# Second attention: transposed scores, attending and outputs of a head one slot later

## What is computed

```python
x = layernorm(x + L0_attn(x))      # 16 heads of 64, keys and values from a latent of 64, causal
x = layernorm(x + L0_ffn(x))       # shared expert + 2 of 16 routed experts
x = layernorm(x + L1_attn(x))      # 16 heads of 16 features; the change is here
x = layernorm(x + L1_ffn(x))       # relu^2, then 5 steps of a spiking neuron, mean of the spikes
```

```python
q_c = rms_norm(xh @ W_DQ.T @ W_UQ.T, q_norm_w); q = concat(q_c, q_c @ W_QR.T)    # 16 + 64
k_c, v = split(xh @ W_DKV.T @ W_UKV.T);         k = concat(rms_norm(k_c, k_norm_w), xh @ W_KR.T)
attn = softmax(q @ k.T * 16**-0.5 + causal);    out = (attn @ v) @ W_O.T
```

## Time and profile before

| | us |
|---|---|
| median of 3 runs | 1758.01 (1756.82 to 1760.86) |
| profiled execution | 1759.73 |
| its span, first to last instruction | 1757.8 |
| PE busy in the span | 1607.7 (91%) |
| DVE busy | 1201.9 (68%) |
| ACT busy | 1015.7 (58%) |
| POOL busy | 461.5 (26%) |
| mean granted TensorE clock | 0.969 of full |

### The profile page before, as it was taken

How to read it: one execution, slowest core, us unless ns; L and a number is a source line. 1 busy time by engine, 2 the same in 40 slices (tenths; PEclk the granted TensorE clock), 3 DMA queues, 4 the chain that set the end, 5 groups by cost and what they waited for, 6 DMA issues and landing times. The chain is left out here.

```text
span 1757.8 us, 29390 instructions
## 1 busy us (share of the span) xinstructions
PE 1607.7 (91%) x9060; PEld 1115.9 (63%) x9060; DVE 1201.9 (68%) x4134; ACT 1015.7 (58%) x2544; POOL 461.5 (26%) x843
## 2 busy tenths in 40 slices
PE   7899999999999999987799976889899988899996
PEld 4667676767677676753588744656556655466765
DVE  1787888888887878755655457788888776125345
ACT  1686766766676767633434364667677766643340
POOL 1000101010101010100275376667676643200001
PEclk9999999999999999998899978999999999999998
DMA  4211111212111111102055528788788786000000
GB/s 107 77 31 47 38 49 43 49 39 52 37 49 43 49 38 40 38 7 96 15 174 162 131 66 155 136 141 150 123 146 134 117 123 119 1 7 24 12 24 30
DMA packets 82632, 128.47 MB, mean 73 GB/s; under 512 B 14640, under 2 KB 40704, under 8 KB 82352
## 3 DMA queue, kind: packets, MB, share of 16 engines
q1 hardware_dynamic: 71232, 100.11, 28.6%
q0 software_dynamic: 9664, 25.93, 5.7%
q10 hardware_dynamic: 1584, 0.55, 0.2%
HBM read 73.59 MB, written 35.65 MB: 62 GB/s over the span
## 5 line engine op out<-in xcount | busy, mean ns | idle before, releaser
L416 ACT ACTIVATE c_probs<-c_probs,a_negmax 128x128 f32<-128x128 f32 (+3 forms) x512 | 279.6, 550 | 0.0
L2004 DVE CUSTOM_DVE_ANT_0 a_junk<-a_ps_score,c_mask 128x128 f32<-128x128 f32 (+3 forms) x512 | 220.3, 487 | 76.1 <-PE a_ps_score L1633 68.2
L1853 ACT ACTIVATE c_probs<-a_ps_st 128x384 f32<-128x384 f32 (+1 forms) x384 | 191.5, 530 | 125.9 <-PE a_ps_st L1655 124.2
L421 ACT ACTIVATE c_probs<-a_ps_trans 128x512 f32<-128x512 f32 (+1 forms) x256 | 124.7, 487 | 215.0 <-PE a_ps_trans L334 214.0
L476 DVE CUSTOM_DVE_ANT_0 c_probs<-a_ps_score,c_mask 128x128 f32<-128x128 f32 (+3 forms) x512 | 219.7, 485 | 19.6 <-PE a_ps_score L318 18.6
L334 PE MATMUL a_ps_trans<-c_ident,c_probs 128*128 128x128 f32 x1280 | 188.7, 278 | 17.8 <-DVE c_probs L493 16.1
L334 PEld LDWEIGHTS a_ps_trans<-c_ident,c_probs 128*128 128x128 f32 x1280 | 147.3, 141 | 87.4 <-issue 39.3
L1655 PE MATMUL a_ps_st<-a_qs,a_ks 128*128 128x512 f32 (+3 forms) x512 | 153.8, 371 | 40.7 <-ACT c_probs L1853 20.4
L539 POOL TENSOR_SCALAR a_rstd<-a_mv 128x4 f32<-128x4 f32 x8 | 1.8, 230 | 704.6 <-DVE a_mv L506 704.6
L317 PE MATMUL a_ps_score<-a_kh,a_qs 128*128 128x128 f32 (+3 forms) x512 | 167.4, 351 | 6.9 <-issue 4.5
L493 DVE TENSOR_SCALAR c_probs<-c_probs,a_recip 128x128 f32<-128x128 f32 (+3 forms) x512 | 164.4, 384 | 4.5
(11 more groups left out here) (273 smaller groups left out, 3156.1 us busy)
## 6 DMA issues: line engine op xcount, KB each, us to landing
a_qs<-a_qlow SPq DMA_DIRECT2D x128, 128.0 KB, 2.2
bounce<-a_words SPq DMA_DIRECT2D x64, 256.0 KB, 6.2
a_qs<-bounce SPq DMA_DIRECT2D x128, 128.0 KB, 5.7
a_ks<-bounce SPq DMA_DIRECT2D x128, 128.0 KB, 6.2
slot_out<-m_y SPq DMA_DIRECT2D x80, 128.0 KB, 2.0
a_xT<-in_xT SPq DMA_DIRECT2D x8, 512.0 KB, 3.8
c_X<-in_x SPq DMA_DIRECT2D x8, 512.0 KB
token_rows<-c_X SPq DMA_DIRECT2D x8, 512.0 KB, 5.7
```

The lines of the kernel that those rows point to most:

```text
L416: act.activation(at, at, ACT.Exp, scale=-1.0, bias=negmax[:, n % 4, i:i + 1], accum_out=rowsum[:, n % 4, i:i + 1]).then_inc(s_exp, 1)
L421: act.activation(probT[:, n % 4, TGCOL[grp]:TGCOL[grp] + TGLEN[grp]], ps_trans[(3 * n + grp) % 2][:, 0:TGLEN[grp]], ACT.Copy).then_inc(s_p ...
L1853: act.activation(probT[:, r8, col:col + width], ps_st[item % 2][:, 0:width], ACT.Exp).then_inc(s_stc, 1)
L2004: dve.tensor_tensor_reduce(out=junk[:, to:to + keys], in0=ps_score[g][:, at:at + keys], in1=C.mask[:, L - keys:L], scale=-1.0, scalar=3.0e ...
```

## The change

`BACK` goes from 7 to 8: the transposed scores of a head, and with them ACT's exponentials and POOL's cut, run eight slots behind its scores. Attending, the copy `yq`, the transposition back and the outputs of a quad are each called one slot later than before, on PE, ACT and DVE. Where SP issues its fills is not edited, but `used(u)` counts items that are now issued a slot later. `turn_max`, `keep_max` and `shifts` stay at slot 4u + 5.

```diff
-BACK = 7
+BACK = 8
@@ PE
-                    if n >= 12 and n % QUAD == 0 and (n - 12) // QUAD < NQUADS:
-                        attend((n - 12) // QUAD, (0,))
-                    if n >= 12 and n % QUAD == 1 and (n - 13) // QUAD < NQUADS:
-                        attend((n - 13) // QUAD, (1, 2, 3))
+                    if n >= 13 and n % QUAD == 1 and (n - 13) // QUAD < NQUADS:
+                        attend((n - 13) // QUAD, (0,))
+                    if n >= 13 and n % QUAD == 2 and (n - 14) // QUAD < NQUADS:
+                        attend((n - 14) // QUAD, (1, 2, 3))
...
-                    if n >= 12 and n % QUAD == 2 and (n - 14) // QUAD < NQUADS:
-                        turn_back((n - 14) // QUAD)
+                    if n >= 13 and n % QUAD == 3 and (n - 15) // QUAD < NQUADS:
+                        turn_back((n - 15) // QUAD)
@@ ACT
-                    if n >= 12 and n % QUAD == 2 and (n - 14) // QUAD < NQUADS:
-                        u = (n - 14) // QUAD
+                    if n >= 13 and n % QUAD == 3 and (n - 15) // QUAD < NQUADS:
+                        u = (n - 15) // QUAD
                         act.wait_ge(s_y, u + 1)
@@ DVE
-                    if n >= 12 and n % QUAD == 3 and (n - 15) // QUAD < NQUADS:
-                        outputs((n - 15) // QUAD)
+                    if n >= 13 and n % QUAD == 0 and (n - 16) // QUAD < NQUADS:
+                        outputs((n - 16) // QUAD)
```

## The result

| | before | changed |
|---|---|---|
| median of 22 runs, us | 1758.82 (1753.79 to 1764.51) | 1765.02 (1760.35 to 1773.44) |
| ratio to before, 95% interval | | 1.0034 [1.0024, 1.0045] |
| profiled execution, us | 1759.73 | 1768.87 |
| its span, us | 1757.8 | 1767.0 |
| PE busy, us | 1607.7 | 1614.4 |

The change costs 6.2 us by the medians and 9.2 by the two spans; the profiled execution of the changed kernel is the second slowest of its 22, whose granted clock has a median of 0.972. The predicted 1759 is missed by 6; 1765.0 lies inside the range of 1745 to 1770. Measured again on another chip the change came out at 1.0014 [0.9997, 1.0030], so its size is uncertain by a few us.

The account below looks back on a forecast made before the run. PE sets the pace, idling for the DMA of the shifts and for ACT. Terms -5.5 - 5 + 0.5 + 6 + 5 - 1.4 + 1.5 = +1.1 us on the median 1758.0 gave 1759 us; range 1745 to 1770.

Parts of the forecast that it names:

- Part 1: Middle of attention: later need for the shifts takes off 5.5 us of waits and 5 of lost clock.
- rival C: Second attention: fill, words and shifts all come a slot later, waits and slow clock stay; +11, 1769 us; chance 0.20.
- Part 2: ACT's queue: the moved yq copy delays copies PE waits for; 0.5 us per eight slots, +6 over 12 periods.
- Part 3: DVE's queue: outputs behind max, means and mix make PE's attend block wait 8 times about 0.6 us, +5.
- Part 4: Start of the stage: PE runs slot 8's scores within the 6.13 us wait, landing unchanged at 1100.8 us; -1.4.
- The late phase: After the front has ended: three quads wait about 1.05 us each for keys, probably one clock drop; net +0.5.
- Part 5: Tail: one head's exponents move there, and ACT waits for the attending of quad 30 in slot 134; +1.5 us.
- B: Relief: shift waits after the start and lost clock behind them end, new holes are half; -13, 1745 us; chance 0.23.
- D: Fills: the 1.3 us margin for a quad's own keys and queries is not there; 1780 us; chance 0.10.
- the signs named ahead: Shift waits behind the start under 2 us, slot 3's hole near 1.0, eight DVE waits about 0.6, three late key waits.
- the clock's one drop: Sign for 1130 to 1420 us: granted TensorE clock at 1.00 but for one drop.

Follow-up runs that it names:

- the other trace: The changed kernel as it is, run and profiled again on another chip: 1.0014 of the kernel before, median 1766.28 us.
- the last version with `BACK` 7: The changed kernel with ACT's yq copy, DVE's outputs and SP's word stores reordered and BACK at 7: 0.9927 of the kernel before, median 1748.65 us.

## Why the prediction was right and wrong, point by point

**Part 1, shift cover and fills: the waits stayed, and this carries the miss.** Predicted -5.5 us of waits and -5 of clock in the middle. Measured: waits 4.7 to 4.4 us, 3.5 in the other trace; clock lost 6.8 to 5.1 us (13.6 and 10.2 us at half clock), 1.7 in the other trace; by the runs with half the loads the two together went from 9.0 to 9.4, in the other trace to 5.7. So 0 to 3.3 us in place of 10.5. The clock is the milder half of this: over all executions on the other chip 7.2 us of it came back in the whole kernel. Why, with the waits hardly smaller, isn't shown.

The step that failed is the claim that a longer period gives the DMA queue time, so that the shift waits go. The queue doesn't run on the period; it runs from a fill's release to the need of the shifts behind it. That is four slots in both kernels. Before: slots 3 to 6, 2.98 + 2.86 + 5.30 + 2.49 = 13.6 us, and 0.7 into the next slot. Changed: slots 4 to 7, 2.14 + 6.15 + 2.91 + 2.52 = 13.7, and 0.7. The period did grow by 1.5 us (25.6 to 27.1): slots 2 and 3 by some 2, slots 0 and 1 shrank by 1.3, and slots 4 to 7 grew by 0.8 to 0.9. But the stretch gave up slot 3, of 2.98 us, for slot 7, of 2.1 to 2.3 before the change, and that took back what slots 4 to 7 had gained.

The DMA side is no shorter than before. SP in the changed kernel and the landing of the shifts of the last row, which answer to the earlier trace rows:

```profile
1335.93 0.50 SPq L1434 DMA_DIRECT2D a_qs<-a_qs  x1
...
1341.33 0.53 SPq L1447 DMA_DIRECT2D a_qs<-a_shift  x1
```

```profile
DMA to landing us min/median/max: 9.2/9.2/9.2
```

The shifts leave earlier behind their fill, 5.4 us after its first issue in place of 6.9, as forecast, and land later, 9.2 us in place of 7.0: 14.6 us in all against 13.9 (medians over the eleven of the middle: 14.1 and 13.6). Leaving earlier was worth nothing here: the same loads and stores stand ahead of them in the queue.

The count of slots orders the other runs too. The four slots take 15.1 us in the run with the old `BACK` (waits in the middle 0.4 us), 13.7 in the changed kernel (4.4), 13.6 in the one before (4.7), 13.4 with ACT's copy moved (5.9), 13.2 with DVE's outputs moved (6.1) and with `BACK` alone (5.3), 12.8 with both moved (7.9), while fill and shifts take 13.6 to 14.1 us wherever their landing is recorded. With the stores behind the shifts that is 12.4 to 12.7 us, and the waits are 0.8 us at 13.6 and none at 12.8; only the last version with `BACK` 7 doesn't fit, with 3.8 us of waits at 13.6 and 12.5.

This is rival C's mechanism, which got 0.20: a price of 11 us was on record for it, its waits "over 5" against 4.1 to 4.7 measured. For its other half, that the slow clock stays, the executions on the other chip speak against it: the 10.0 us apart from the clock are near C's price, but 7.2 us of lost clock come off.

The rule named in the prediction for C, the Trainium skill, DMA: Bandwidth & Descriptors, section Queues, rings and completion order, says that a DMA's step of the semaphore lands only after the earlier writes on its engine. The traces agree: 8 KB land in 1.8 us at the least and 8.7 at the most in the middle of the kernel before, in 9.2 and 10.1 us behind a fill and two stores in the changed one, and in 3.8 to 5.6 us in the changed one with half the loads.

**Part 2, ACT's order: right.** Predicted a hole of 1.04 us in slot 3; measured 1.03. Predicted that the second hole of slot 7 keeps 0.5 us; measured 0.34, and slot 7, which now holds the turn-back of 0.6 too, grew by 0.27 to 0.40 us. Of the 1.07 us of attending that leave slot 4, 0.65 were to come back: it went from 2.86 to 2.14 us, 0.7.

**Part 3, DVE's order: right.** Predicted eight waits of 0.4 to 0.9 us, 5 us; measured 8, 5.9 us, two sizes, 0.49 and 0.96. Parts 2 and 3 were to cost 5.5 and 5 us in the 11 periods from slot 16 to 104 and cost 11.5 together by the pair with half the loads.

**Part 4, the start: the size was off.** Predicted -1.4; measured -3.2 and -3.6. The exponents start at 1100.8 us in both kernels, as forecast; PE in order of time, answering to the first of the earlier trace rows, and then the kernel before:

```profile
1099.16 1.54 PE L1633 MATMUL a_ps_score<-a_ks,a_qs 128*128 128x128 f32 x4 [3.98 <-DMA a_ks<-bounce]
1100.81 1.12 PE L1655 MATMUL a_ps_st<-a_qs,a_ks 128*128 128x512 f32 x2
```

```profile
1102.77 1.48 PE L1633 MATMUL a_ps_score<-a_ks,a_qs 128*128 128x128 f32 x4
```

Slot 8's scores did not run inside the 6.13 us wait, as I had it; they wait for keys that land at 1099.2 and then run directly ahead of the exponents. In the kernel before they come behind them, for 1.48 us: that is the -1.4. The forecast left out that up to slot 16 the exponents of one head fewer are issued, some 1 us at the full clock and up to 1.8 at the lower one (1.11 and 0.69 in the first head of the kernel before). The two make about -3. The second of them is no gain of the kernel: these exponents are in the tail.

**The late phase: the size was off, on the good side.** Predicted three waits of 1.05 us for keys, one drop of the clock at 3 us, and +0.5 us in all; measured waits of 0.36, 0.89 and

```profile
1477.37 0.90 PE L1633 MATMUL a_ps_score<-a_ks,a_qs 128*128 128x128 f32 x4 [2.10 <-DMA a_ks<-bounce]
```

3.4 us in all, which is the +3.2 of the forecast. But from slot 104 to 127 the stretch became 2.9 us shorter (3.7 in the other trace). The waits for shifts there fell from 4.5 us to 0.3 and the half clock from 6.8 us to 3.4, of which the wait of 2.10 us is followed by one. 3.4 - 4.2 - 1.7 = -2.5. The forecast had priced the drop at nearly twice what it cost.

**Part 5, the tail: the size was right.** Predicted +1.5, measured +3.0 and +2.0, and +2.0 in the pair with half the loads. The first holds 1.7 us of lost clock that the kernel before doesn't have there. PE's window of the changed kernel:

```profile
1510.00:1520.00 10.00, 7.41 (x23) 3.71 (x21) 1.11 (x3) 6.59 (x14) 1.62 (x4) 0.85 0.00 1
```

Without it +1.3, and the other trace, with the clock at 1.00 throughout the tail, has +2.0. The wait behind it is there too; ACT in order of time, and nothing like it in the kernel before:

```profile
1528.72 0.60 ACT L1265 ACTIVATE a_xs<-a_ps_score 128x512 f32<-128x512 f32 x1 [2.69 <-PE a_ps_y L1671]
```

It is 2.7 us and not 1.5, since ACT also waits out the products ahead of the attending. That it is what makes the +2 was not shown: taking it away made the tail longer. The rival, the exponents of the one head more that the tail now holds (some 1 us of PE), was not tested apart from it.

**Sum.** By the predicted parts: middle +0.5 (11 less 10.5), start -1.4, late +0.5, tail +1.5, +1.1. By the two traces: middle +11.9, of which orders 11.5 and DMA and clock +0.4; start -3.2; late -2.9; tail +3.0, 1.7 of it clock; rest +0.4; +9.2. The medians on that chip give 6.2. The other trace gives -3.6 + 8.2 - 3.7 + 2.0 = +2.9, and the ratio on its chip, 1.0014, is +2.6. That 1765 lies within the range is in part luck: the middle came out some 8 to 11 us worse than forecast, and the start and the late stretch 5 to 6 us better.

**The rivals.** B had the orders at half their cost and no clock lost: both wrong. D decided from a landing of 12.7 us; keys came in time in the middle, with no wait between 1126 and 1420 us, so no, though the last load of one quad in two landed 11.3 to 12.7 us after the fill's first issue. It was waiting behind the repairs, though: in the version with both orders mended and the stores moved the scores wait for keys four times in the middle too, where the period is shorter and the release as late. Of the signs named ahead, the hole of slot 3, the eight waits for DVE and the three late waits for keys came as written; the shift waits did not. Of the clock's one drop three came in this trace, at 1128, 1213 and 1312 us, and one in the other, at 1337.

## What to carry over

Before one stage of a software pipeline is moved to cover a DMA, count the slots from what releases the transfers ahead of it to the need for it, and see which of them grow: if release and need move together, the cover changes only by the slots that enter and leave that stretch, whatever the period does. Where small urgent transfers share a queue with bulk stores, try them ahead of the stores first: moving two lines of SP's order gave 0.66% alone, twice what the change lost, and on the changed kernel, with the moved copy put behind the copies that PE waits for and the moved outputs ahead of means and mix, it gave 0.93%. A moved instruction that costs nothing in its old slot has a price in the new one that can be read off in the rows: see what it is then ahead of in its queue, and who waits for that.

## What the runs showed that was not expected

- The issue time of the shifts hardly sets their landing: in the changed kernel they left 1.5 us earlier behind the fill and landed 0.7 us later after it.
- With half the loads the DMA engines' share falls from 0.82 to 0.47 and the granted clock of the middle is 1.00 throughout in both kernels; with all of them it fell to half for 3.4 or 6.8 us at a time (1.7 or 3.4 us lost). Of the six drops in the middle of the kernel before and the first changed trace four stand behind waits of 1.35 to 1.73 us for a DMA. One, at 1393 us of the kernel before, stands behind holes of 0.59 and 0.57 us, and one, at 1312 us of the changed kernel, behind nothing longer than 0.53 us: the attend block below takes 1.94 us where it takes 1.06 at the full clock. And the version with both orders mended has nine shift waits of up to 1.4 us in the middle and no drop there. In the tail the clock fell even in the runs with half the loads. Where it falls differs from trace to trace, and one drop is worth as much as most terms of the sum.

```profile
1312.19 1.94 PE L1671 MATMUL a_ps_y<-c_probs,a_v 128*32 128x512 f32 x8 [0.50 <-DVE a_yq L2016]
```

- The releaser that a row names can be a bystander: "DVE a_negmax" for the third item of slot 7 (4.5 us x13) stands where ACT's chain made the hole of 0.57 us before; when ACT's order was mended, these waits went to ACT's name again (3.2 us x6) and DVE was nowhere.
- The same kernel's median differs by 11 us from chip to chip (1758.8 to 1769.8), more than any effect of the change.
